# Four order tables and two shared PSUM banks laid anew in a hand-ordered attention and mixture-of-depths kernel

## The reference

```python
q, k, v = heads(x @ w_q.T), heads(x @ w_k.T), heads(x @ w_v.T)      # 16 heads of 8
s = einsum('bhqd,bhkd->bhqk', rms_norm(q), rms_norm(k)) / sqrt(8)
s = tanh(s / 50) * 50                                               # soft cap
p = softmax(where(causal, s, -inf))
x1 = layernorm(x + merge(einsum('bhqk,bhkd->bhqd', p, v)) @ w_o.T)

weights = x1 @ router_w + router_b                                  # one number per row
topv, topi = top_k(weights, 64)
sel_mask = weights > topv[:, -1]
idx = sort(topi[:, :63])                                            # 63 rows of each batch
xs, m = x1[idx], attention_mask[idx, idx]
q, k = rope(rmsnorm(xs, ln1) @ wq), rope(rmsnorm(xs, ln1) @ wk)     # positions of the rows
a = softmax(q k^T / sqrt(8) + m) v, 16 heads
x1f = xs + a @ wo
x2 = x1f + gelu(rmsnorm(x1f, ln2) @ w1) @ w2
y = zeros.at[idx].set(x2 * weights[idx]) + x1 * (1 - sel_mask)
out = layernorm(x1 + y)
```

## Time and profile before

| | |
|---|---|
| device time of the runs | 833.2, 833.04 and 830.16 us, median 833.04 us |
| the profiled execution | 828.81 us, its span 825.8 us |
| busy PE, PEld | 624.4 us (76%), 365.3 us (44%) |
| busy DVE, ACT, POOL | 596.5 (72%), 549.7 (67%), 395.6 us (48%) |
| mean granted clock of TensorE | 0.82 |
| tanh and exp on ACT (L763, L774) | 278.0 and 271.6 us |
| scores and PV on PE (L1231, L1250) | 130.2 and 155.8 us |
| HBM read and written | 14.69 and 4.19 MB |

### The profile page before, as it was taken

How to read it: one execution, slowest core, us unless ns; L and a number is a source line. 1 busy time by engine, 2 the same in 40 slices (tenths; PEclk the granted TensorE clock), 3 DMA queues, 4 the chain that set the end, 5 groups by cost and what they waited for, 6 DMA issues and landing times.

```text
span 825.8 us, 16681 instructions
## 1 busy us (share of the span) xinstructions
PE 624.4 (76%) x6576; PEld 365.3 (44%) x6576; DVE 596.5 (72%) x1681; ACT 549.7 (67%) x403; POOL 395.6 (48%) x399
## 2 busy tenths in 40 slices
...
GB/s 191 64 50 29 64 15 64 14 46 136 25 53 2 129 3 76 27 66 13 77 12 80 14 64 16 59 46 5 61 27 64 2 64 28 13 1 26 0 0 51
DMA packets 96910, 36.72 MB, mean 44 GB/s; under 512 B 68018, under 2 KB 94146, under 8 KB 96834
## 3 DMA queue, kind: packets, MB, share of 16 engines
...
HBM read 14.69 MB, written 4.19 MB: 23 GB/s over the span
## 4 chain that ended last, share of the span: by engine, by line
PE 46%; DVE 23%; ACT 13%; issue 12%; POOL 5%; POOLq 0%; DVEq 0%
PE ps_y L1250 15%; ACT pr L763 8%; PE ps_s L1231 5%; ACT pr L774 4%; POOL k_wide L663 4%; PE ps_a L1281 3%; PE ps_m L1281 3%; PE ps_m L1407 2%; DVE wins L989 2%; PE ps_a L1444 2%; PE ps_m L1309 2%; PE ps_a L1309 2%; PE ps_m L1257 2%; DVE v_aug L887 2%; PE ps_m L1359 1%
## 5 line engine op out<-in xcount | busy, mean ns | idle before, releaser
L763 ACT ACTIVATE pr<-ps_s 128x1024 f32<-128x1024 f32 (+1 forms) x256 | 278.0, 1128 | 121.8 <-PE ps_s L1231 81.6
L774 ACT ACTIVATE pr<-pr 128x2304 f32<-128x2304 f32 x128 | 271.6, 2122 | 1.8
L654 POOL TENSOR_TENSOR pr<-pr,tri 128x256 f32<-128x256 f32 (+2 forms) x192 | 145.6, 775 | 173.8 <-ACT pr L774 173.8
L1231 PE MATMUL ps_s<-q_st,k_st 32*64 32x512 f16 (+7 forms) x2048 | 130.2, 328 | 49.0 <-ACT pr L763 45.3
L1250 PE MATMUL ps_y<-pr,v_aug 128*32 128x512 f32 (+7 forms) x2048 | 155.8, 439 | 1.1 <-POOL pr L661 1.1
L1231 PEld LDWEIGHTS ps_s<-q_st,k_st 32*64 32x64 f16 x2048 | 52.5, 111 | 123.0 <-ACT pr L763 53.9
L675 POOL TENSOR_TENSOR st<-qk,st 128x1024 f16<-128x1024 f32 x32 | 73.9, 2328 | 35.2 <-DVE st L903 35.2
L1250 PEld LDWEIGHTS ps_y<-pr,v_aug 128*32 128x32 f32 x2048 | 57.8, 113 | 70.2 <-issue 49.9
L663 POOL TENSOR_TENSOR k_wide<-qkT,head_of 128x1024 f32<-128x1024 f32 x16 | 30.1, 1902 | 61.8 <-DVE qkT L1072 61.8
L661 POOL TENSOR_TENSOR pr<-pr,tri 128x256 f32<-128x256 f32 x64 | 54.2, 847 | 0.0
L663 POOL TENSOR_TENSOR r<-x,rw_row 128x512 f32<-128x512 f32 x16 | 18.9, 1180 | 65.5 <-DVE x L965 65.5
...
## 6 DMA issues: line engine op xcount, KB each, us to landing
...
q_st<-st SPq DMA_TRANSPOSE x16, 4.5
k_st<-st SPq DMA_TRANSPOSE x16, 4.7
```

The source lines that it names most:

```text
L654: return nc.gpsimd.tensor_tensor(buf, buf, tri[:, None, :].to_broadcast([P, blocks, 64]), ALU.mult)
L763: nc.scalar.activation(slots[:, first:first + step + 1:step, c0:c1], ps_s[:, p0:p0 + 2 * n].rearrange("p (m c) -> p m c", m=2), ACT.Tanh, ...
L774: nc.scalar.activation(slots[:, slot(n), :], slots[:, slot(n), :], ACT.Exp, scale=SOFTCAP)\
L1231: last = mm(ps_s[64 * s:64 * s + 64, col:col + S - 64 * kb], k_st[rows, k, gi // 2, 64 * kb:64 * kb + 64], q_st[rows, k, gi // 2, 64 * kb: ...
```

## The change

No operation is added, removed or changed. What changes is the order in which PE, DVE and POOL do the steps of the sides, the bank that each use takes with the readers that it waits for, and how the last passes are laid out. The parts:

- `PE_ORDER`, `VE_ORDER` and `POOL_ORDER` are filled anew: nearly every step stands in another half step, and some in another pass (`late.ln` of a pair moves from shift -3 to -2, `att.sc0` from the start of one pass to the end of the one before, likewise `sel.msel` and `route.coef/1` on DVE and `fin.y0T/1` and `route.thr/1` on PE). `ACT_ORDER` keeps its entries.
- `BANK` and `BANK_READ` are filled to suit.
- The passes with tables now end with p = 7. The one step that is left of the frame follows, and then the rest of the last two pairs from four flat lists, `PE_LAST`, `VE_LAST`, `POOL_LAST` and `ACT_LAST`, with banks and readers of their own (`BANK_LAST`, `BANK_READ_LAST`; a key is `use@unit`, the pair counted from behind). `at` takes the unit for this reason, and so do its callers.

The ring of `pr`, the frame, and SP's list are as before.

```diff
 PE_ORDER = (
...
-    ["att.wo@-2", "route.wrow/0@-1"], ["att.h2T@-2"],
-    [], ["prep.xT/0@1", "att.w1@-2"],
-    ["route.won/0@-1", "prep.qk0/0@1", "prep.qk1/0@1"], ["fin.y0T/0@0", "pv.4/0@0", "route.wrow/1@-1"],
...
+    ["route.wrow/0@-1", "prep.qk0/0@1"], ["prep.qk1/0@1", "att.h2T@-2"],
+    [], ["att.w1@-2"],
+    ["route.won/0@-1", "fin.y0T/0@0"], ["route.wrow/1@-1", "pv.4/0@0"],
...
 POOL_ORDER = (
+    [], ["prep.sq/1@0"],
     ["sel.zb@-2", "route.xw/0@-1"], [],
-    ["prep.sq/1@0"], [],
...
+PE_LAST = (
+    "att.S0@-2", "pv.4/1@-1", "pv.5/1@-1", "att.S1@-2", "pv.6/1@-1", "pv.7/1@-1", "fin.y1T/1@-1", "att.P0@-2",
+    "fin.yT/1@-1", "att.P1@-2", "fin.wo/1@-1", "att.PV@-2", "att.oT@-2", "att.wo@-2", "route.wrow/0@-1",
...
 BANK = {
     "att.P0": "a",
-    "att.P1": "a",
+    "att.P1": "m",
     "att.PV": "a",
-    "att.S0": "m",
+    "att.S0": "a",
     "att.S1": "m",
...
 BANK_READ = {
...
-    "att.h2T": ["att.x1f@0"],
+    "att.h2T": ["att.oT@0", "prep.qk0/0@3"],
...
-        def at(use, unit=None):
-            return {"a": ps_a, "m": ps_m}[BANK[use if unit is None else f"{use}/{unit.k}"]]
+        def at(use, unit):
+            key, pair = (f"{use}/{unit.k}", unit.pair) if isinstance(unit, Batch) else (use, unit)
+            return banks[BANK_LAST.get(last_use(key, pair), BANK[key])]
...
-        def iterations(body):
-
-            for p in range(-1, PAIRS + 3):
-                body(p)
...
+        def iterations(body, last, table):
+
+            for p in range(-1, PAIRS):
+                body(p, range(16))
+            body(PAIRS, range(1))
+            run_side(last, table, PAIRS)
...
             def bank_free(use, unit):
 
-                pair = unit.pair if isinstance(unit, Batch) else unit
-                for reader in BANK_READ[use if not isinstance(unit, Batch) else f"{use}/{unit.k}"]:
+                key, pair = (f"{use}/{unit.k}", unit.pair) if isinstance(unit, Batch) else (use, unit)
+                for reader in BANK_READ_LAST.get(last_use(key, pair), BANK_READ[key]):
```

More of the change, by code:

```diff
@@ L143 @@
[L143 to L149, removed]
+    ["prep.qk0/1@0"], ["prep.qk1/1@0", "att.S0@-2"],
```

415 lines of the change are left out of this document (270 added, 145 removed).

## The result

The changed kernel takes **914.13 us** (median of four runs, 910.39 to 915.53) against 832.51 us for the kernel before: a ratio of 1.0978, 95% interval 1.095 to 1.1005. The forecast was 795 us in a range of 766 to 820. It is wrong in sign and by far.

The account below looks back on a forecast made before the run. No engine is full; PE's row, 75.27 us busy plus 13.09 idle, was taken to set a pair. Gains 19 + 9 + 3 + 7 = 38 us gave 791 profiled, 795 us for the runs, range 766 to 820.

Parts of the forecast that it names:

- The step that failed: Four full pairs: only PE's idle time and slow stretches change; each step starts at its engine's turn or its inputs.
- The lower bound of a pair: Full pairs: DVE's 72.12 us of work and some 3 us of waits, 75 us.
- four full pairs: Pairs with the pipeline full: 83 us each, 19 us less over the four, through shorter PE waits and less slow clock.
- the first three: Pairs while the pipeline fills: 9 us less together, as score waits go; bounds 3 and 15.
- the eighth: Last pair, with no next pair to prepare: some 60% of a full pair's gain, 3 us less; bounds 0 and 6.
- the tail: After the last exp, the last pair's chain in a new order: 7 us less; bounds 0 and 12.
- The clock: PE in full pairs: shorter idle pieces let the slow clock cost 5 us instead of 8; granted clock 0.9 or more.
- The rival with the clock at full speed: Waits shrink and PE's clock stays up: 78 us a full pair, 65 us less in all, 768 us; chance 0.20.
- That POOL holds back the masks: Rival: xw/0 waits for a later x1/0 ahead of the causal products, delaying pv.0; slower, 841 us; chance 0.06.
- None of the four: Rivals for the whole kernel: clock stays up 768 us, waits change places 818, POOL delays masks 841, no telling change 833.
- the waits for the ring of buffers: First three pairs: tanh waits for PV to free probability buffers, 40.1 us in eleven waits; to stay but for some 2 us.
- ACT's wait for `hu`: Full pairs: ACT waits 2.33 us for POOL's hu; to stay, since DVE still does w/1 ahead of hp.

Follow-up runs that it names:

- the two runs with fills: Kernel before and changed kernel, each with every POOL instruction after setup replaced by two constant fills of the same output: 815.96 us and 792.22 us.
- the form with one tensor input: Changed kernel in its own order, with the 128x1 roots of sel and att taking their second number as a scalar per partition: 885.44 us.
- the second version: Changed kernel with DVE's table relaid to miss POOL's work, scalar-form roots in sel and att, and two POOL steps moved: 866.72 us.

## Why the prediction was wrong

*The step that failed* stands at the head of the full pairs: "No step is added, so only PE's idle time and its slow stretches can change", and with it the laying of "each step at the later of its engine's turn and its inputs". It takes the work of DVE as fixed, as if an operation lasted as long in its new place as in the old one. For DVE's small operations, the duration in the trace of before is one in a certain place: away from POOL's instructions. In their new places they last up to thirteen times as long (2.10 us in place of 0.16), and no term of the sum, no bound and no rival had this. The lower bound of a pair was even built on "DVE's 72.12 us of work", which became 90.33. That this is the cause is shown by the two runs with fills, where 122 us go with POOL's reading, and by the form with one tensor input, where 29 us go with nothing else changed.

*The forecast of the order was right in sign, too large, and not for its reasons.* With fills on both sides, so that only the order differs, the terms are: four full pairs 15.4 us less (342.30 to 326.92; forecast 19), the first three 3.9 less (245.8 to 241.9; forecast 9), the eighth 0.8 less (forecast 3), the tail 3.8 less (forecast 7). That is 24 us against 38. Of the five microseconds that a pair was to gain, three were to come from the clock and two from shorter waits. With fills PE's work in the four pairs stays as it was (296.2 and 297.0 us, at clocks of 0.88 and 0.87), so the clock gave nothing; PE's idle time fell from 46.1 to 29.9 us, 4 us in a pair. A full pair takes 81.7 us where 83 had been laid, and 792 us meets the forecast of 795, but that is chance: the fills also take away the 17 us that the lock costs the old order.

*The clock* was forecast to rise with a denser row, from 0.86 to 0.9 in the sixth pair. It fell to 0.81, while PE's idle time grew; with fills PE idles for only 6.4 us in that pair, and the clock is 0.85 all the same. The rival with the clock at full speed no run here shows. One of its grounds was misread: the clock of 0.50 does not come "only behind the waits of rows 3". The third stretch of the earlier trace rows, from 527.8, follows 20.5 us in which PE was busy for 17.07 at a clock of 1.00, and the idle time right ahead of it, 1.38 us, is none of those rows.

*The rivals.* That POOL holds back the masks had the right engine and the wrong mechanism. PE waited for POOL ahead of `pv` for 7 us in the whole run, and not at all in the four full pairs. None of the four was what happened, though the sign and the price of "slower" were at hand: the profile of before has an operation on four numbers per partition that takes 944 ns on average, and its timeline shows one such, `route.w/0`, right behind the CAST that sets `lo/1` off. In the changed kernel, in another place, the same operation takes 0.23 us each time.

```profile
L974 DVE TENSOR_SCALAR x<-x,rb 128x4 f32<-128x4 f32 x16 | 15.1, 944 | 0.6
```

```profile
485.39 0.69 DVE L903 CAST st<-qk 128x1024 f16<-128x1024 f32 x1
...
486.71 1.39 DVE L974 TENSOR_SCALAR x<-x,rb 128x4 f32<-128x4 f32 x1
```

The Trainium skill has the rule too (SBUF — State Buffer, "Who interferes with whom"): VectorE and GpSimd share a second pair of SBUF ports, a VectorE instruction with two SBUF inputs contends with a GpSimd instruction that reads SBUF but not with one that only writes, and whoever comes second is blocked until the first has ended. The runs agree at each point: 2.1 us under a product of POOL, 0.15 us under a fill, 0.21 us with one tensor input, and `sq/0` above, which came second itself and took 2.34 us. The page adds that copies, casts and scalar forms in a mode with two ports contend with GpSimd too. Two operations with one tensor input would fit that: `w` above, and `sel.hn`, at 1.10 us under a fill against 0.28 in the changed kernel outside of POOL's work. In which mode they ran, no run here shows. The rule on two SBUF inputs spoke against the change, and the prediction did not weigh it.

*What else came out:* the waits for the ring of buffers stayed, eleven in the first three pairs as in the earlier trace rows. DVE no longer waits 3.65 us ahead of `ET`, as forecast, but in the changed kernel it is late there itself; with fills it waits 1.0 us. ACT's wait for `hu` was to stay at 2.3 us and fell to 1.0. A wait for `mx1` (`pm`) came that the prediction did not have. ACT's waits in the sixth pair of the changed kernel:

```profile
ACT pr L895 <- PE ps_s L1363: 25.5, 16, 3.8
ACT pm L868 <- DVE pm L1218: 3.3, 1, 3.3
ACT hq L872 <- POOL hu L795: 1.0, 1, 1.0
```

*What stays open:* why one microsecond of lock costs more in one place than in another. In the second version 69 us of time went with 66 us of DVE's work (624.5 to 558.7 us busy over the span); in the changed kernel 122 us with 153 (713.2 to 560.1).
